# Fewer and wider products of zeros in a recurrence on TensorE, its side work split over two steps, and fillers behind the loop and the transposes

## The reference

```
# 1. a recurrence over 512 steps, for 8 sequences at once
xw = x @ Wx + b
h[t] = tanh(xw[t] + h[t-1] @ Wh)          # 256x256 weights, 8 rows per step
# 2. a long convolution of h, kernel K from a sum of exponentials, plus h * D
K = sum_n C_re[:, n] * exp(dt * A[n] * t)
x = x + (causal_conv(h, K) + h * D)
# 3. a gated scan (sigmoid gates, two cumulative sums), then a shared MLP
#    and 16 experts of 320 rows, top 2 of 16, scattered and gathered
x = x + (hid + shared_mlp(hid) + experts(hid)), hid = gated_scan(x)
```

## Time and profile before

| | us |
|---|---|
| median of 3 runs | 973.68 |
| the three runs | 973.1, 973.68, 978.77 |
| the profiled execution, its own time | 974.19 |
| its span | 972.3 |
| TensorE busy in the span | 924.3 |
| TensorE busy with the products of zeros in the loop (L489) | 141.1 |

### The profile page before, as it was taken

How to read it: one execution, slowest core, us unless ns; L and a number is a source line. 1 busy time by engine, 2 the same in 40 slices (tenths; PEclk the granted TensorE clock), 3 DMA queues, 4 the chain that set the end, 5 groups by cost and what they waited for, 6 DMA issues and landing times.

```text
span 972.3 us, 64880 instructions
## 1 busy us (share of the span) xinstructions
PE 924.3 (95%) x28864; PEld 777.5 (80%) x28864; DVE 410.7 (42%) x781; ACT 506.3 (52%) x1735; POOL 299.1 (31%) x324
## 2 busy tenths in 40 slices
PE   7999999999999999999999998999899999999993
PEld 5888888888888888996444446788899999999993
DVE  1000010100001103553899799875564646556450
ACT  2444444444444446443876587134465656566551
POOL 3111111111111110650003463760045364554545
PEclk6799999999999999999999999999999999999997
DMA  2222222221111111111001110533357666675634
GB/s 89 83 92 87 95 93 87 100 85 33 35 40 36 35 33 28 66 76 57 0 1 39 49 56 22 184 116 108 127 132 162 133 157 119 151 146 127 134 40 53
DMA packets 69161, 80.34 MB, mean 83 GB/s; under 512 B 24225, under 2 KB 53558, under 8 KB 69122
## 3 DMA queue, kind: packets, MB, share of 16 engines
q1 hardware_dynamic: 54242, 62.18, 20.3%
q0 software_dynamic: 14592, 17.10, 10.7%
q10 hardware_dynamic: 288, 0.56, 0.2%
HBM read 44.16 MB, written 33.83 MB: 80 GB/s over the span
## 4 chain that ended last, share of the span: by engine, by line
PE 81%; issue 5%; ACT 4%; POOL 4%; DVE 3%; DMA 2%; POOLq 0%; SPq 0%; ACTq 0%; DVEq 0%
PE ps L516 19%; PE ps L811 16%; PE ps L508 9%; PE ps L825 8%; PE ps L677 8%; PE ps L489 6%; PE ps L727 3%; POOL slots_in L447 2%; PE ps L577 2%; ACT tok L879 2%; PE ps L590 2%; PE ps L736 2%; PE ps L599 2%; PE ps L494 2%; DMA slots_in<-tok,arena 1%
## 5 line engine op out<-in xcount | busy, mean ns | idle before, releaser
L516 PE MATMUL ps<-tok,wh 128*32 128x8 f32 x16384 | 255.2, 180 | 12.9 <-issue 3.5
L879 ACT ACTIVATE tok<-ps 128x8 f32<-128x8 f32 x1024 | 155.9, 177 | 204.0 <-PE ps L516 201.6
L516 PEld LDWEIGHTS ps<-tok,wh 128*32 128x32 f32 x16384 | 220.0, 113 | 48.0 <-ACT tok L879 25.2
L466 POOL DMA_INDIRECT out<-arena,dest x80 | 127.9, 1599 | 99.3 <-ACT arena L1030 76.9
L489 PE MATMUL ps<-zero 128*32 128x192 bf16 x1920 | 141.1, 255 | 0.0
L418 POOL TENSOR_TENSOR big<-tok,zero 128x128 f32 x64 | 29.0, 453 | 322.0 <-ACT tok L879 322.0
L811 PE MATMUL ps<-xgT_hi,ew_hi 128*128 128x320 f32 (+1 forms) x384 | 119.5, 311 | 3.2 <-DVE spare L1275 1.6
L811 PE MATMUL ps<-xgT_hi,ew_lo 128*128 128x320 f32 (+1 forms) x384 | 119.5, 311 | 0.0
L811 PE MATMUL ps<-xgT_lo,ew_hi 128*128 128x320 f32 (+1 forms) x384 | 119.0, 310 | 0.0
L1143 DVE TENSOR_TENSOR arena<-arena,pack 128x256 f32 x32 | 13.6, 426 | 246.3 <-ACT arena L884 246.3
L1381 DVE TENSOR_TENSOR mid<-mid,ps 128x320 f32<-128x320 f32 (+1 forms) x96 | 46.6, 486 | 107.0 <-ACT mid L1048 57.5
(11 more groups left out here) (206 smaller groups left out, 1643.5 us busy)
## 6 DMA issues: line engine op xcount, KB each, us to landing
slots_in<-mid SPq DMA_DIRECT2D x16, 645.0 KB, 3.7
mid<-slots_in SPq DMA_DIRECT2D x16, 645.0 KB, 4.2
arena<-in_ex_down SPq DMA_DIRECT2D x16, 384.0 KB
arena<-in_ex_gate SPq DMA_DIRECT2D x16, 352.0 KB
arena<-in_ex_up SPq DMA_DIRECT2D x16, 352.0 KB
xst<-in_x_steps SPq DMA_DIRECT2D x66, 64.0 KB, 1.8
xtok<-in_x_tok SPq DMA_DIRECT2D x16, 256.0 KB, 2.7
mid<-k_pad SPq DMA_DIRECT2D x32, 128.0 KB, 3.1
```

The source lines that it names most:

```text
L466: pool.indirect_dma_start(out=out[:, :], out_offset=bass.IndirectOffsetOnAxis(ap=dest[:, z, t:t + 1], axis=0), in_=yo[:, z, t], in_offset= ...
L516: last = nc.tensor.matmul(sums_at(bank, t, o)[Q * j:Q * j + Q], wh[:, k, columns(j, o)], hring[:, (n - 1) % (2 * G), k], start=False, stop ...
L879: nc.scalar.activation(hring[:, n, o], sums_at(n // G, n % G, o), ACT.Tanh).then_inc(s_h[o], 1)
```

## The change

- In the loop, zeros stand behind seven of the 16 steps, n = 0, 2, 4, 6, 10, 12 and 14, with 320 columns each; before they stood behind 15 steps with 192 columns.
- `kernel_sums` is cut in two halves of four records each; the first stands behind n = 7, the second behind n = 8 (`G` is 8), and `s_kmm` comes with the second. A wait for `s_ps0` in front of it, which TensorE has already passed ahead of the loop, is left out.
- Behind the loop, ahead of the wait for `s_hist`, stand 28 products of zeros of 128 by 8 columns over the whole array.
- Behind the 64 transposes, ahead of the waits for their copies, stand five products of zeros of 512 columns over the whole array.

```diff
-            def kernel_sums():
-
-                for c in range(KP):
+            def kernel_sums(half):
+
+                for c in range(KP // 2 * half, KP // 2 * half + KP // 2):
                     last = nc.tensor.matmul(ps[0:C * KP, 4, 0:HB], cblk[:, c], kq[:, c], start=c == 0, stop=c == KP - 1, skip_group_check=True, tile_position=(0, 0))
-                last.then_inc(s_kmm, 1)
+                if half == 1:
+                    last.then_inc(s_kmm, 1)
...
-                    if n != G - 1:
-                        keep_groups_up(192)
+                    if n in (0, 2, 4, 6, 10, 12, 14):
+                        keep_groups_up(320)
                     if n == G - 1:
-                        pe.wait_ge(s_ps0, 1)
                         pe.wait_ge(s_kqe, i + 1)
                         pe.wait_ge(s_kc, i + 1)
-                        kernel_sums()
+                        kernel_sums(0)
+                    if n == G:
+                        kernel_sums(1)
...
+            for _ in range(28):
+                keep_up(8)
             pe.wait_ge(s_hist, 2 * IT + 2)
...
                 last.then_inc(s_utr, 1)
+            for _ in range(5):
+                keep_up(512)
```

## The result

The kernel after the change takes 964.09 us as the median of five runs (963.19 to 999.63), and the kernel before 974.13 in its five: a ratio of 0.989, with a 95% interval of 0.985 to 0.993. The forecast was 963.4 us. In some executions of most variants, the 999.63 among them, the clock of TensorE is at 0.50 through the convolution, which makes them 30 to 40 us longer, and the ratios are made without them where a kernel has both kinds. The profiles of runs 2, 3, 4, 5 and 9 show this fall; elsewhere it is read from the time and from a mean clock of 0.93 to 0.95.

The account below looks back on a forecast made before the run. TensorE's program was taken as the path, with only loop step time over 0.67 us recoverable. From 974.19, minus 11.6, plus 1.3 and 0.3, gave 964.2; run-median and dip adjustments (0.51, 0.3) gave 963.4 us, range 960 to 978 (8 in 10).

Parts of the forecast that it names:

- the floor: Loop: shortest distance between Tanh pairs, 0.67 us, the round PE, ACT, PE; only time above it can be won back.
- the small products: 28 fillers behind the loop: 0.045 us each taken, 1.3 us against a gap of about 1.0, so 0.3 us lost.
- The loop: Full-clock part of the loop: 0.38 us gained per turn over 30.5 turns, 11.6 us in all.
- n = 7 and 8: Loop steps with the split kernel sums: excess of 0.17 us goes, 0.16 taken per turn, nothing added behind n = 8.
- n = 1 and 9: Loop steps losing their zeros: from 0.74 to 0.675 us, 0.065 gained each, 0.13 per turn.
- n = 2 and 10: Loop steps with zeros widened to 320 columns: 0.012 us lost each, 0.02 per turn.
- The turn of the loop: Step n = 15, zeros removed ahead of the loop's branch: 0.03 us gained per turn, bounds 0 and 0.04.
- The low-clock start: First turns at 1.2 GHz: fewer zeros make the clock rise 5 us later, 1.3 us lost.
- The wide products: Five fillers behind the transposes: 1.07 us inside a wait of 1.16, nothing lost; 0.9 lost were the clock low.
- The dip: Low-clock stretch at 694 to 697 us may fall on idle time: worth up to 0.8 us, 0.3 gained taken.
- The rival with the low loop: Whole loop stays at 1.2 GHz because fewer zeros never raise the clock: 107 us lost, 1080 us; chance 0.08.
- The next wait: Rival in the loop: bias row's clearing time replaces the zeros' wait, only the sums' split pays, 4.9, 969 us; chance 0.11.

Follow-up runs that it names:

- run 2: Kernel before with only the zeros changed (320 columns behind seven steps), sums whole, no fillers; five of six executions 998 to 1006 us, the sixth 965.36.
- run 3: Changed kernel without the 28 small and five wide filler products behind the recurrence; 1000.37 us, ratio 1.025.
- run 4: Changed kernel without any zeros in the loop, fillers kept; 1077.16 us, ratio 1.104.
- run 5: Changed kernel with its 33 filler products replaced in place by 66 waits on a long-passed semaphore; five of five at 1001 to 1006 us.
- run 9: Changed kernel without fillers, 66 waits put far ahead of the loop; three of five at 997 to 999 us, two at 963.45 and 965.54.
- run 1: Kernel before with only the kernel sums split over n = 7 and n = 8; ratio 0.994, 968.39 us at best, three of seven at 1006 to 1008.
- run 8: Changed kernel with zeros widened to 512 columns behind n = 0 and 448 behind n = 4, 6, 12 and 14; 963.46 us, ratio 0.987.
- run 10: Changed kernel with four wide products for the 28 small ones, plus 48 waits ahead of the loop; one of six at 1001 us, others 963.81 to 969.55.
- run 12: Changed kernel without fillers, 128 waits put far ahead of the loop; 964.38 us, ratio 0.990, none of seven near 1000.

## Why the prediction was right, and where it wasn't

The mechanism of the gain was right: each wait over the floor is a term of its own, and the terms add up. The closeness of the total, 963.4 against 964.09, is in part luck: 1.6 us was set aside for a later rise and for the small products, which cost almost nothing, and a dip in the gates, for which nothing was set aside, took 1.7.

- *The loop.* 12.06 us where 11.6 was summed. The terms, from ACT's rows before and after: n = 7 and 8 0.16 (0.16 taken; run 1 has it by itself), n = 1 and 9 0.07 each (0.065), n = 3, 5, 11 and 13 0.02 each (0.02). Behind n = 2 and 10 nothing was lost where 0.012 was taken. The turn of the loop is the term that moves: the excess over the floor had a median near 0.13 before and 0.06 after, and between turns and kernels it was anything from none to 0.17.
- *The low-clock start.* 1.3 us was set aside for a later rise. In the profile the rise was at 35.9, and 35.1 in the kernel before, so some 0.2 us was lost. In single executions it does come later: run 1 has it at 51.8, run 8 at 47.7. A rise 12 us later is worth 3 us by the 0.26 of the earlier trace rows, which is about the scatter of 963 to 967.
- *The small products.* 0.045 us each was taken, and it was 0.025 ((0.85 - 0.18) / 27), so all of them were hidden and 0.3 too much was charged. The Trainium skill's floor for starts (TensorE: Matmul & The Clock Gate, "Wait — 56ns, not 53.3ns?"), named in the prediction for this very case, agrees with the trace; bounds from rows of other kinds were 0.013 and 0.11.
- *The wide products.* Nothing, as said.
- *The dip.* Its place moved, as said, but not for the better: 1.7 us lost in the gates and 0.5 won behind them, where 0.3 won was taken.
- *The rival with the low loop* had its place and mechanism right: without zeros the clock never rises in the loop. That 1080 us was worked out and 1077 measured is luck. A turn was taken at 14.7 us and takes 13.4, so the loop adds 62 us to that of the kernel before and not 107, and 35 more come from the low convolution, which the prediction didn't have. At 320 columns the low loop doesn't come about; at 192 the clock rises late in some executions, if it rises at all.
- *The next wait* was wrong: the products start 0.24 behind the bias row (150.00 and 150.24 behind n = 1), as that rival had it, but this is just the floor's start, and the step is 0.003 over the floor.
- *What the prediction hadn't seen at all.* It priced the cover of the fillers at 0.9 us and asked only whether they fit. The fall of the clock in the convolution costs 36 us, since the convolution never brings it back, and what shifts the odds is not work in the array but where a 16 KB piece of code begins. The part on the loop took 64 instructions out and never asked what lies behind them. Without the 28 products as ballast the forecast would have been wrong by 36 us: that is runs 2 and 3, in 11 of 12 executions. The prediction took them for fillers of a gap, so this part of the hit is luck as well.

Open: in run 9 the boundary is by the same count at the 61st or 62nd of 64 transposes, and the load still came late; in run 10 it was third from last and came in time. In run 5 it lies by the same count among the 36 waits, still ahead of TensorE's wait for the copies, and the load came late as well. Where exactly the edge is wasn't settled. That the load is asked for when TensorE's program comes up to the boundary is inferred from these counts, and no record shows it. Nor is it known why the pause brings the clock down in most executions and not in all, or why the excess at the turn of the loop varies.

## What to carry to other kernels

Taking instructions out of a hardware loop, or adding them, moves all code behind it against the 16 KB pieces in which it is loaded; look in the trace for pauses with "issue" as their releaser and for the load ahead of them, and if a pause has grown, shift the code by waits in a place where the engine idles anyway, and run again. Judge fillers by taking them away in two ways, once with their work and once with their instruction count kept. And price a fall of TensorE's clock by how long the stage behind it can't bring it back, not by the gap; take at least five executions, since the median of three may hide an outcome of one in five.

## What the runs showed of the hardware that was not expected

- At 1.2 GHz the convolution, with TensorE busy for 88.4 of 90 us in run 3, is not granted the full clock; the same code at 2.4 GHz keeps it (run 12 and others). In the five profiles of a fall the clock rises 6 to 8.5 us behind the convolution's end, in the gates.
- A load of 16 KB of code takes 0.9 to 1.8 us (one took 2.4), and in the convolution the products that need it start 2.2 to 2.8 us behind its start. No two loads start less than 3.4 us apart. Where the first load behind the loop is late, the second is too: 14.5 to 17.2 us behind the loop's end, and 13.1 to 13.3 elsewhere.
- 66 waits on a semaphore take the place of about 33 instructions of code, and 128 of about 64.
- Small products over the whole array with bf16 weights of 128 columns start 0.025 us apart.
